# Graph network in one kernel: the exchange of target keys put ahead of the records' assembly, the runs by target one sort level earlier, six groups of picks ahead of TensorE's first turn of the sort

## The reference, cut to what matters

```python
def _segment_sum(src, seg, n):
    return jax.ops.segment_sum(src, seg, n)
...
    edge_index = jnp.stack([src, dst])
    h = jnp.maximum(_layernorm(x, axis=-1), 0.0)
    x = x + _L0_gnn_ref(h, src, dst, edge_weight, L0_gnn_weight, L0_gnn_bias)
    h = jnp.maximum(_layernorm(x, axis=-1), 0.0)
    x = x + _L1_gnn_ref(h, edge_index, edge_type_8, L1_gnn_W1, L1_gnn_b1, ...)
    h = jnp.maximum(_layernorm(x, axis=-1), 0.0)
    x = x + _L2_gnn_ref(h, edge_index, L2_gnn_hyperedge_weight, L2_gnn_W, L2_gnn_b)
    h = jnp.maximum(_layernorm(x, axis=-1), 0.0)
    x = x + _L3_gnn_ref(h, node_vec1, node_vec1_n2, src, dst, edge_attr_4, edge_attr_8, ...)
    return x
```

## Time and profile before

| | us |
|---|---|
| median of 3 runs | 3288.9 (3285.91 to 3291.98) |
| the profiled execution, its own time | 3285.04 |
| its span in the profile | 3283.2 |
| POOL busy | 2419.0 (74%) |
| DVE busy | 1930.4 (59%) |
| PE busy | 1725.3 (53%) |
| ACT busy | 1078.9 (33%) |
| end of the last dense chunk on DVE, line 457 | 518.0 |
| last gather of line 703 on POOL | 635.2 |
| last add of stage 2 on POOL | 1007.4 |

### The profile page before, as it was taken

The page is one execution under the profiler, slowest core; times in us unless marked ns, Lnnn a source line. Parts: engine busy times, 40 slices in busy tenths (PEclk is TensorE's granted clock), DMA queues, the critical chain, the costliest instruction groups (busy, mean ns, idle before and its releaser), DMA issues.

```text
span 3283.2 us, 39195 instructions
## 1 busy us (share of the span) xinstructions
PE 1725.3 (53%) x7779; PEld 1276.3 (39%) x7779; DVE 1930.4 (59%) x6186; ACT 1078.9 (33%) x2956; POOL 2419.0 (74%) x2038
## 2 busy tenths in 40 slices
PE   0344004888812555564484335777676745555553
PEld 0343003777710212221363333555454435545453
DVE  5885446887812555555896775433333357666664
ACT  0332004675612444443354554222222222121210
POOL 4477687788887777773366775888888878888887
PEclk9865556998955877666555555666767677776676
DMA  7699996355642222221463554655655556555554
GB/s 171 189 314 358 341 356 183 74 62 83 116 38 53 80 79 79 80 79 55 136 216 113 130 129 105 126 114 114 115 113 113 110 122 130 114 116 113 113 116 73
DMA packets 423455, 436.96 MB, mean 133 GB/s; under 512 B 55330, under 2 KB 348883, under 8 KB 423061
## 3 DMA queue, kind: packets, MB, share of 16 engines
q0 software_dynamic: 128576, 130.98, 25.5%
q1 hardware_dynamic: 237472, 240.03, 23.8%
q10 hardware_dynamic: 57336, 65.24, 6.9%
HBM read 248.75 MB, written 187.31 MB: 133 GB/s over the span
## 4 chain that ended last, share of the span: by engine, by line
POOL 30%; issue 11%; DVE 5%; PE 4%; ACT 2%; DMA 1%; ACTq 1%; DVEq 0%; SPq 0%; POOLq 0%
POOL out_dram L717 18%; POOL work L703 12%; DVE work L2092 2%; PE bank L934 1%; ACT work L1316 1%; PE bank L1029 1%; DVE work L1896 0%; DMA work<-he,idx_last_s 0%; PE bank L1107 0%; ACT work L1417 0%; DVE work L2129 0%; DVE work L2130 0%; PE bank L1093 0%; DVE work L2128 0%; PE bank L1037 0%
## 5 line engine op out<-in xcount | busy, mean ns | idle before, releaser
L1896 DVE TENSOR_TENSOR_SCAN work<-work,bank 128x512 f32<-128x512 bf16 (+1 forms) x294 | 364.0, 1264 | 318.5 <-PE bank L934 290.1
L717 POOL DMA_INDIRECT out_dram<-work,idx_add_s x196 | 312.4, 1594 | 65.2 <-issue 57.6
L717 POOL DMA_INDIRECT out_dram<-big,idx_add_s x196 | 310.4, 1584 | 62.4 <-issue 54.5
L717 POOL DMA_INDIRECT out_dram<-big,idx_add_d x196 | 312.3, 1593 | 59.7 <-issue 59.1
L1309 ACT ACTIVATE work<-work,eps_col 128x4 f32<-128x4 f32 (+1 forms) x196 | 58.5, 298 | 734.0 <-DVE work L1872 733.9
L703 POOL DMA_INDIRECT big<-x_by_edge,idx_e_s x196 | 215.1, 1098 | 74.6 <-issue 59.4
L993 PE MATMUL bank<-ident,work 128*128 128x128 f32 x392 | 88.2, 399 | 332.6 <-ACT work L1316 332.6
L934 PE MATMUL bank<-ident,work 128*128 128x128 f32 x392 | 103.5, 415 | 297.5 <-ACT work L1316 171.7
L1316 ACT ACTIVATE work<-work 128x128 f32<-128x128 f32 x588 | 236.7, 480 | 50.7 <-DVE work L1891 50.7
L703 POOL DMA_INDIRECT work<-he,idx_last_s x196 | 191.4, 977 | 75.7 <-issue 59.4
L703 POOL DMA_INDIRECT work<-d,idx_run_d x196 | 188.2, 960 | 75.4 <-issue 59.4
(11 more groups left out here) (362 smaller groups left out, 5381.6 us busy)
## 6 DMA issues: line engine op xcount, KB each, us to landing
out_dram<-work SPq DMA_DIRECT2D x57, 726.0 KB, 9.0
work<-in_x_dram SPq DMA_DIRECT2D x57, 704.0 KB, 10.2
edge_w<-work SPq DMA_DIRECT2D x49, 512.0 KB, 2.7
work<-edge_w ACTq DMA_DIRECT2D x49, 512.0 KB, 3.8
work<-flags_src SPq DMA_DIRECT2D x98, 128.0 KB
gat_h<-work SPq DMA_DIRECT2D x49, 256.0 KB
work<-flags_dst SPq DMA_DIRECT2D x98, 128.0 KB
work<-gat_h SPq DMA_DIRECT2D x49, 256.0 KB
```

Of the source, the lines that this page charges most:

```text
L717: g_.indirect_dma_start(table[:, :], bass.IndirectOffsetOnAxis(ap=of[:, at_:at_ + 1], axis=0), row, None, compute_op=ALU.add).then_inc(add ...
L1896: return V.tensor_tensor_scan(to, flag_b[G.place][rows, :], of, before if G.from_(1) else 0.0, ALU.mult, ALU.add)
```

## The change

Three things are moved. On ACT the exchange of the target keys and the loads of the neighbours stand right behind the raw loads' issue, ahead of the records' assembly (in the branch that is taken for sorted targets). On DVE the runs block comes after level 5 and no longer waits for the assembly or the records; the copy of the edge weight with its wait goes to the end of level 6. Six groups are found by PE before its first turn of the sort, and picked by DVE two each after levels 6, 7 and 8; the groups that follow are shifted by six, so 15 are left after the sort instead of 21, and the six dense chunks that stood beside the other six follow without a pick.

```diff
-RUNS_AT = 6
+RUNS_AT = 5
...
-LATE = 28
+FIRST = 6
+LATE = FIRST + 28
...
             def find_two(j):
-                find(2 * j)
-                find(2 * j + 1)
+                find(FIRST + 2 * j)
+                find(FIRST + 2 * j + 1)
+            for g in range(FIRST):
+                find(g)
             sort_transposes(find_two)
...
+            unsorted = load_unsorted(act)
+            with act.If(unsorted < 1):
+                exchange_keys("dst", 1, 1)
+                neighbours("dst", 1)
             act.wait_ge(ids_in, 16 * 9)
             act.wait_ge(raw_in, 16 * 9)
             act.wait_ge(dense_ready, 1)
...
-            unsorted = load_unsorted(act)
             with act.If(unsorted > 0):
                 keep_records("BY_DST", rec, REC)
                 act.wait_ge(R["taken"], NG)
                 act.sem_inc(raw_stored, 16)
+                exchange_keys("dst", 1, 1)
+                neighbours("dst", 1)
...
-            exchange_keys("dst", 1, 1)
-            neighbours("dst", 1)
             act.wait_ge(src_ready, 1)
...
+                if 6 <= k <= 8:
+                    if k == 6:
+                        dve.wait_ge(raw_stored, 32)
+                        link(V.tensor_copy(edge_c[:, :, 0], rec3[:, :, R_W]))
+                    pick(picks[1])
+                    pick(picks[1] + 1)
+                    picks[1] += 2
...
                 dve.wait_ge(keys_in, 32)
-                dve.wait_ge(rec_ready, 1)
                 run_flags(keyl, prevl, nextl, "dst")
...
-                dve.wait_ge(raw_stored, 32)
-                done(V.tensor_copy(edge_c[:, :, 0], rec3[:, :, R_W]))
...
-            assert n + 1 == STRAIGHT * DBUF
+            for n in range(AHEAD_CHUNKS + NG - LATE, STRAIGHT * DBUF):
+                dense_chunk(V, dve, n // DBUF, n % DBUF)
             dense_steps(STRAIGHT, STRAIGHT + 2)
```

More of the change, by code:

```diff
@@ L1202, in _, with exchange_keys, neighbours @@
                               ).then_inc(raw_in, 16)
+            def exchange_keys(which, n_keys, n_done):
+                act.wait_ge(keys_ready, n_keys)
+                k = keys_dram[which]
+                act.dma_start(k[1:EP + 1].rearrange("(q f) -> q f", f=F), keyl).then_inc(keys_stored, 16)
+                act.dma_start(k[0:1].unsqueeze(0), edge_mark[0:1, 0:1]).then_inc(keys_stored, 16)
+                act.dma_start(k[EP + 1:EP + 2].unsqueeze(0), edge_mark[0:1, 1:2]).then_inc(keys_stored, 16)
+                act.wait_ge(keys_stored, 48 * n_done + 16 * (n_done - 1))
+            def neighbours(which, n):
+                k = keys_dram[which]
+                act.dma_start(prevl, k[0:EP].rearrange("(q f) -> q f", f=F)).then_inc(keys_in, 16)
+                act.dma_start(nextl, k[2:EP + 2].rearrange("(q f) -> q f", f=F)).then_inc(keys_in, 16)
+                act.wait_ge(keys_in, 32 * n)
+            unsorted = load_unsorted(act)
+            with act.If(unsorted < 1):
+                exchange_keys("dst", 1, 1)
+                neighbours("dst", 1)
             act.wait_ge(ids_in, 16 * 9)
@@ L1233, in _ @@
                               rec_raw.rearrange("(t p) c -> p t c", p=P)).then_inc(raw_stored, 16)
[L1235 to L1248, removed]
             def store_flags(which, n):
```

## The result

The kernel after takes **3260.7 us** (median of 4 runs, 3255.4 to 3262.5) against 3289.1 us before (4 runs, 3285.9 to 3292.0): a ratio of 0.9909, 95% interval 0.9897 to 0.9922. The forecast was 3258 with a range of 3250 to 3270. The profiled execution took 3261.0 us with a span of 3259.2, 24.0 us less than the span of before; the medians are 28.4 apart, since the profiled execution of before lay 4 us under its median and that of after 0.3 us above its own. POOL's lines 703, 717 and 749 are now 704, 718 and 750; the low parts' store is now line 1269, the key stores lines 1210 to 1212, the store of source ids line 1264, `hot` lines 1278 to 1282, the pick line 1840.

The account below looks back on a forecast made before the run. POOL's single string of work, starting at 114.15 us, was taken as the bound. (114.15 - 85.1) + 1.2 = 30.2 us off the median 3288.9 gave 3258.7, taken as 3258, range 3250 to 3270.

Parts of the forecast that it names:

- The bound: POOL is one string of work from 114 to 1009 us; each us of earlier start is a us of the kernel.
- The fourth rival: Another engine, held by something unseen, ends stage 1 or 2; gain within noise, 3289 us; chance 0.03.
- The stall moves and shortens: ACT's queue: the stall passes from the keys' store to the source ids' store, released at 66 us.
- S: Time at which ACT's queue releases the store of source ids: 66 us, bounds 60 and 73.
- the first rival: The records' load stalls ACT's queue the full 29.5 us again; S = 73, gain 23, 3266 us; chance 0.15.
- The exchange: ACT's early key stores and neighbours' loads: neighbours in at 26 us, bounds 24.5 and 43; DVE needs them at 48.2.
- the third rival: Neighbours' loads wait out big loads of x until 43; S = 99.6, POOL resumes at 118.7, 3293 us; chance 0.03.
- From S to the restart: `hot(0)` done at S + 8.3, three finds 6.2 more, landed store 4.6 more: POOL resumes at 85.1 us.
- the second rival: DMA transfers set the ring's pace from 150 us, so the earlier start fills idle time; 3280 us; chance 0.06.
- Runs at level 5: DVE's runs block, 24.4 us less the weight copy, runs from 48.2 to 72.3; level 6 ends at 76.3.
- all 71 chunks run inside POOL's string before and after: Stage 1's dense chunks on DVE: their cost to POOL's string was claimed to stay unchanged.
- less than 25 us: Sign of a wrong bound: POOL restarts at 85 but its last stage 2 add is less than 25 us earlier.

Follow-up runs that it names:

- e1: Kernel before with only the key exchange and neighbours' loads moved ahead of the records' assembly: 3270.6 us, ratio 0.9948.
- e2: Changed kernel with the exchange and neighbours' loads put back behind the records' load on ACT: 3277.7 us, ratio 0.9964.
- e3: Changed kernel with the runs block back after level 6, exchange and six groups of picks still ahead: 3257.6 us, ratio 0.9904.
- e8: Changed kernel with the records' load issued from SP's queue and the dense chunks' constants read from PSUM: 3201.5 us, ratio 0.9751.
- e9: Kernel before with only the dense chunks' addition reading its constant from PSUM: 3250.1 us, ratio 0.9878.
- e10: Same kernel as e6, measured again on the same chip as e9: 3209.2 us, ratio 0.9754.
- e6: Changed kernel with the dense chunks' addition reading its constants from a PSUM copy instead of SBUF: 3206.5 us, ratio 0.9757.

## Why the prediction was right

**The bound.** Right. POOL is one string from its restart to the end of stage 2, and five kernels with restarts from 81.9 to 105.4 had their times shifted with it. The fourth rival (something else ends the string) falls.

**The stall moves and shortens.** Right: S was forecast at 66 and is 65.6; the first rival (29.5 us at full length, S = 73) falls. The argument was that the same transfers fill the same time, in whatever order, and the runs bear it out more widely than the prediction claimed: the load was issued by ACT between 32.1 and 44.0, and the queue was released at 64.6 before, 65.6 after, 65.1 in e1, 66.7 in e2 and 64.8 in e3. The length of the stall, 33.7 to 20.8 us, is just what is left until then.

**The exchange.** The neighbours were in at 27.4 (26 forecast, bounds 24.5 and 43), so the third rival falls. By the Trainium skill's rule on completions, weighed in the prediction, S would have been 83 and the restart 102. That delay didn't come. The rule isn't refuted by it: the neighbours' loads were issued at 23.55 and 23.91, when the engines were 0.27 busy (22 to 24 us; 0.77 from 24 to 27.4, 1.16 from 28 on), and no run here issues them into the full stretch. In rival 3's sum S comes to 99.4 and not 99.6, and the restart to 118.5, which changes nothing there.

**From S to the restart.** Small errors cancelled in part, which is luck. From S to the end of `hot(0)` it took 10.0 us (74.91 + 0.72 - 65.62), not 8.3: the source ids needed 3.2 us to land instead of 1.7. From there to the start of `hot(4)` at 80.98 it took 5.35 us, not 6.2. The prediction filled that stretch with PE's finds at 2 us each; five groups took 7.40 us, 1.5 each, and what set the pace was mostly ACT itself, one group's one-hot every 1.37 us and a single wait of 0.63 us for PE. From `hot(4)` to the landed store it was 5.0 us for 4.6. Restart 86.0 against 85.1; the ask for the first turn 96.6 against 95.2; the runs block ended at 73.6 for 72.3. No ring wait followed, and the second rival (DMA gives the start back) falls: at 1.07 of share and 335 GB/s the shift held until 331.67, 331 forecast.

**Runs at level 5.** It was costed as work that fits in either place, without a gain of its own. e3 confirms it: none.

**The step that failed**, in a forecast that was otherwise right, is the sentence that all 71 chunks run inside POOL's string before and after, "so what they cost it stays". Their number stays; what they cost doesn't. Of the 71, three fall into POOL's wait ahead of line 703 in either kernel. The string of line 703 began 30 us earlier while the last chunk ended only 11 us earlier, so 37 fell into it instead of 33 and its gathers took 5.0 us more. The first string had 31 in place of 35 and gave back only 1.6 (181.7 us of gathers before, 180.1 after). The balance, 3.4 us, is most of the 4.6 us by which the last add came late (981.6, 977 forecast). The prediction asked for "less than 25 us" there as the sign of a wrong bound; it was 25.8 (1007.4 - 981.6), 0.8 us short of calling a right bound wrong.

**The sum.** 30.2 us were forecast. The medians give 28.4, the two profiled executions 24.0; single executions of the kernel after lie 7 us apart, and those of e8 11, so the first is the better measure. From the median the forecast was 3258.7, and 3260.7 came out.

**Not seen at all** was what else the six early picks did: the last pick moved by 41 us, from 338.0 to 297.0. It is worth nothing in this pair of kernels, and some 12 us in POOL's wait ahead of the second string as soon as POOL is faster (31.0 in e9, 18.8 in e10).

## What to carry to other kernels

When one engine is a single string of work, price a change at the wait that starts the string, and then ask what lies beside the shifted string: work with a clock of its own overlaps other parts of it than before. The stall in ACT's queue behind a load of many small pieces was here the rest of that load's time, with the DMA engines full until it ended: moving the issue by 12 us changed the stall's length and not its end, so what others wait for belongs ahead of such a load. And read the mean of the bound engine's commonest instruction: a 1.12 us gather whose undisturbed neighbours take 0.94 was worth 54 us and one operand moved to PSUM, twice what this change brought.

## What the hardware did that was not expected

**A DVE addition with two SBUF inputs holds POOL's indirect gathers.** The 128x1408 fp32 addition takes 1.62 us; a gather that starts within it ends 0.81 to 0.83 us behind its end, after 1.22 to 2.40 us instead of 0.94, while one that is already under way isn't held (51 of 53 under 1 us). Over the 392 gathers of stage 1 the excess was 57.5 us before and 61.7 after. With one input in PSUM it is 2.5, of which 0.1 is in the second string, at the same length of the addition (1.61 us). The Trainium skill (SBUF — State Buffer, Who interferes with whom) says that a DVE instruction with two SBUF inputs contends with a GpSimd instruction that reads SBUF; a gather reads its indices there, and e6, e9 and e10 agree. The same section infers that `tensor_tensor` doesn't stall the generation of descriptors. These runs show that it does hold the instruction that issues them; whether at the reading of the indices or at the writing of descriptors, none of them separates.

**A single load can hold its issuer's queue for 20 to 34 us**, in which the next `dma_start` of that engine doesn't return, here 20.77, 21.56 and 33.74 us behind the load of the records in pieces of 64 bytes (29.53 in the kernel before). Issued from SP, the same load left ACT's queue free (0.34 us), but the store of the low parts beside it took 8.4 us to land instead of 1.6. Whether SP's queue hung in turn isn't shown: SP had nothing else to issue from 46.2 to 108.9 us.
